# A graph layer with an expert layer on Trainium2: dividing, turning and measuring final node tiles between the last edge batches

## The chip, the cores and the metric

The kernel runs on one core of a Trainium2 chip. The metric is the device time of one execution in microseconds. The kernel before took 1845.05 us, the median of three runs from 1842.29 to 1846.93.

## The reference

`x` is 6250 nodes by 256. `src` and `dst` hold 106250 edges, sorted by `dst`, self-loops among them. What is computed, shortened:

```python
def _L0_gnn_ref(x, edge_index, W, att_src, att_dst, bias, gamma, beta):
    xh = (x @ W).reshape(N, H, D)
    e = leaky_relu(a_src[src] + a_dst[dst], 0.2)
    e = exp(e - segment_max(e, dst)[dst])
    alpha = e / segment_sum(e, dst)[dst]
    out = segment_sum(xh[src] * alpha[:, :, None], dst).reshape(N, H * D) + bias
    out = (out - mean(out, axis=0)) * rsqrt(var(out, axis=0) + 1e-5) * gamma + beta
    return out + x
...
x = x + _L0_gnn_ref(_layernorm(x), edge_index, ...)
x = x + _L0_ffn_ref(_layernorm(x), Wr, br, ln_g, ln_b, W1, b1, W2, b2)   # 8 experts, top 2
```

The kernel sums the weighted messages and the weights of a node side by side and divides once per node. The norm needs mean and variance of every column over all 6250 nodes, so nothing behind it starts before the last node is known.

## The kernel before

**Tiles.** 6250 nodes are `NT` = 49 tiles of 128 (the last has 106). `acc` in SBUF holds for each tile 256 sums and 8 weight sums (`ROW` = 264). The edges are cut into `USED` = 464 slots of 256 edges (`COUPLE` = 2 tiles of 128), each for one node tile; `SB` = 4 slots are a batch and there are `BATCHES` = 116. A node tile n is final when `CT` + n slots (`CT` = 416) have been added, whatever the data.

**One edge batch b.** GpSimd gathers rows of `node_table` by indirect DMA (L1230), eight gathers of 128 rows to a tile batch, 832 in all, into a ring of `GB` = 4; it waits until the messages of the rows that it overwrites are made. SyncE turns landed gathers into `rows_landed` (L1451) and loads the target rows (L1437). VectorE scores the batch (`score`, L1272 to L1282), sums the picks of the next (L1259), and then makes a message (L1290) and adds an older slot to `acc` (L1254) in turn, four times; adds run `ADDS_BEHIND` = 3 slots behind. ScalarE, once the batch is scored, makes two exponentials (L1418, L1423), the one-hot tile `onehotT` of batch b+2 (L1389, L1383) and the one-hot tile `onehot` of batch b+1 (L1397, L1383). TensorE multiplies the one-hot tile with the messages, four products a slot (L1372), and then makes the picks of batch b+2 (L1348). Ahead of each batch's products and between its slots it runs 16 products on a spare bank, `keep_clock` (L1337). Batches 4 to 99 also carry the splitting of the expert weights.

**Division.** In groups of 7 tiles, as soon as a group is final: VectorE takes the reciprocal of the weight sums (L1307) and, for the first five groups, multiplies (L1244, `multiply`). Groups 5 and 6 are multiplied by GpSimd behind its last gather. The first five divisions lie behind batches 106, 107, 109, 111 and 113.

**The norm.** Behind the last batch TensorE transposes `acc` in 13 chunks of four tiles (`CHUNK`; the last has one tile), eight transposes of 128x128 to a chunk (L1606), into three pairs of PSUM banks in turn (`TURNS`). VectorE takes bn_stats of each half chunk (L1546), ScalarE copies it back to `acc` turned (L1621). Then VectorE aggregates and works out scale and shift (L1553 to L1576); from L1564 on it needs `stage3_rows`, five loads that SyncE issues behind `wait_edges`, which waits for the last add, among others (L1521 to L1524, `bias`, `gamma`, `beta`, `x_logits`, `br`, with the loads of x into `r_ring`, L2096, around them). `wait_edges` also stands ahead of the copies of ScalarE and ahead of the iotas and memsets of GpSimd (L1638 to L1666), which VectorE needs at L1568. TensorE runs 20 `keep_clock` products, spreads the shift (L1611, L1612), runs 8 more and starts x1 (L1997, L2000), tile by tile, with VectorE (L1680, L1685) and ScalarE (L1530, L2036) behind it. Route, rows and the experts follow.

Each engine works through its own instructions in the order of the code; between engines only semaphores order the work.

## Time and profile before

| | |
|---|---|
| median of three runs | 1845.05 us |
| the profiled execution | 1842.22 us, span 1840.3 us |
| mean granted clock of TensorE | 0.943 |
| busy: TensorE, VectorE, ScalarE, GpSimd | 90%, 71%, 62%, 63% of the span |
| score of batch 105, 115 | starts at 1040.8, 1134.3 us |
| last add to `acc` | ends at 1143.0 us |
| the 26 bn_stats of the norm | 1143.4 to 1158.2 us |
| first x1 product | 1165.3 us |
| first expert product | 1252.5 us |

Times of a trace count from the span's start. The profile gives the busy time of each engine, groups of instructions by line, the waits with what ended them, the timeline, and the chain of work that ended last, followed back from the last instruction. PE is TensorE's matmuls and PEld its weight loads, DVE is VectorE, ACT ScalarE, POOL GpSimd, SP SyncE (SPq its DMA issues and waits). A granted clock of 1.00 is 2.4 GHz, 0.50 is 1.2 GHz.

### The profile page before, as it was taken

The page shows a single profiled execution, that of the slowest core. Times are in us where ns is not written, and L with a number is a line of the kernel's source. Part 1 is how long each engine was busy: PE and PEld are TensorE (multiplying, and loading weights), DVE is VectorE, ACT ScalarE, POOL GpSimd, SP SyncE. Part 2 cuts the span into 40 slices and gives each one's busy share as a digit, 9 for nine tenths or more (in the row PEclk, how much of TensorE's full clock was granted, in tenths as well). Part 3 has the DMA queues.
Part 4 walks back from the last instruction along what each step waited for, and adds up shares of the span by engine and source line. Part 5 has one row for each costly group of instructions (what it writes and reads, how often), then busy time and mean ns, then how long its engine had stood idle before and what let it go on. Part 6 is the DMA issues. An engine that isn't in the chain of part 4 may idle for free. (4 is left out here: it accounts for less than half of the span.)

```text
span 1840.3 us, 38213 instructions
## 1 busy us (share of the span) xinstructions
PE 1652.0 (90%) x11100; PEld 1228.8 (67%) x11100; DVE 1300.6 (71%) x3391; ACT 1150.2 (62%) x2503; POOL 1160.1 (63%) x1086
## 2 busy tenths in 40 slices
PE   6588979899897989999899879938999999999997
PEld 4445656566565656665665546717989999999996
DVE  6675858778685876867688768996666666666664
ACT  3665858788695976878697756863444343443443
POOL 1277777777777777777777776004666666556643
PEclk9888979999897998999899989959999999999998
DMA  8645555645555554555655444772333333323322
GB/s 298 226 125 146 146 165 146 170 124 165 151 148 166 144 154 135 155 160 150 167 148 146 124 113 122 257 304 71 54 51 48 49 53 51 51 48 51 51 42 33
DMA packets 122669, 235.10 MB, mean 128 GB/s; under 512 B 23452, under 2 KB 83112, under 8 KB 121288
## 3 DMA queue, kind: packets, MB, share of 16 engines
q0 software_dynamic: 60288, 141.01, 32.6%
q1 hardware_dynamic: 53276, 81.89, 13.4%
q10 hardware_dynamic: 8908, 9.75, 1.6%
q8 instruction: 103, 1.69, 0.4%
q14 instruction: 94, 0.77, 0.1%
HBM read 189.96 MB, written 43.44 MB: 127 GB/s over the span
## 5 line engine op out<-in xcount | busy, mean ns | idle before, releaser
L1230 POOL DMA_INDIRECT gather_ring<-node_table,src_tile x832 | 794.3, 955 | 261.6 <-issue 239.8
L1372 PE MATMUL bank<-message_ring,onehot 128*128 128x264 f32 x1856 | 509.6, 398 | 35.5 <-DVE message_ring L1290 35.5
L1337 PE MATMUL bank<-ones 128*128 128x512 bf16 x1900 | 511.8, 393 | 32.8 <-ACT message_ring L1423 20.7
L1372 PEld LDWEIGHTS bank<-message_ring,onehot 128*128 128x128 f32 x1856 | 356.4, 195 | 160.3 <-DVE message_ring L1290 68.7
L2366 POOL DMA_INDIRECT out_rows<-y,token_idx x105 | 203.9, 1942 | 215.9 <-DMA out_rows<-y,token_idx 156.4
L1337 PEld LDWEIGHTS bank<-ones 128*128 128x128 bf16 x1900 | 181.1, 100 | 219.7 <-issue 50.9
L1290 DVE TENSOR_TENSOR message_ring<-gather_ring,bank 128x512 f32<-128x512 f32 x464 | 315.4, 680 | 3.7 <-ACT bank L1418 1.1
L2334 ACT ACTIVATE hid<-bank,cols 128x256 f32<-128x256 f32 (+1 forms) x448 | 210.4, 551 | 147.3 <-PE bank L2274 144.4
L2274 PE MATMUL bank<-xe,w_hi 128*128 128x256 f16 (+1 forms) x1792 | 283.2, 266 | 0.9 <-DVE xe L2196 0.6
L1397 ACT ACTIVATE onehot<-iota_free,neg_dst 128x128 f32<-128x128 f32 x928 | 282.0, 386 | 0.5 <-PE bank L1372 0.5
L2291 PE MATMUL bank<-w,hid_hi 128*128 x1680 | 278.2, 273 | 0.0
L2274 PE MATMUL bank<-xe,w_lo 128*128 128x256 f16 (+1 forms) x896 | 235.5, 266 | 0.0
L2291 PE MATMUL bank<-w,hid_lo 128*128 x840 | 229.0, 273 | 0.0
L2344 POOL DMA_INDIRECT xs<-x_rows,token_idx x105 | 141.3, 1346 | 117.4 <-DVE token_idx L1978 85.7
L1254 DVE TENSOR_TENSOR acc<-acc,bank 128x264 f32 x464 | 196.0, 422 | 8.7 <-PE bank L1372 8.4
L2205 DVE TENSOR_SCALAR hid_hi<-hid,cols 128x1024 f16<-128x1024 f32 (+1 forms) x112 | 90.2, 805 | 145.5 <-ACT hid L2334 145.3
L2274 PEld LDWEIGHTS bank<-xe,w_hi 128*128 x1792 | 168.5, 98 | 21.7 <-issue 1.7
L1389 ACT ACTIVATE onehotT<-dst_row,minus_one_up 128x1024 bf16<-128x1024 uint8 x116 | 132.2, 1139 | 80.8 <-DMA dst_row<-dst_rows 80.8
L2291 PEld LDWEIGHTS bank<-w,hid_hi 128*128 128x128 f16 x1680 | 164.3, 98 | 20.1 <-issue 0.8
L2318 ACT ACTIVATE xe<-bank 128x512 f16<-128x512 f32 (+1 forms) x56 | 32.0, 571 | 195.4 <-PE bank L2255 195.4
L2208 DVE SCALAR_TENSOR_TENSOR hid_lo<-hid,cols,hid_hi 128x1024 f16<-128x1024 f32 (+1 forms) x112 | 136.4, 1218 | 4.0
L1383 ACT ACTIVATE onehot<-onehot,ones 128x1024 f32<-128x1024 f32 x116 | 133.2, 1149 | 3.8
(336 smaller groups left out, 1771.6 us busy)
## 6 DMA issues: line engine op xcount, KB each, us to landing
stage<-in_L_ffn_W SPq DMA_DIRECT2D x16, 1024.0 KB, 6.0
dst_row<-dst_rows SPq DMA_DIRECT2D x116, 128.0 KB, 3.5
gather_ring<-node_table,src_tile POOLq DMA_INDIRECT x832
w_split<-w_out SPq DMA_DIRECT2D x32, 256.0 KB
w<-w_split SPq DMA_DIRECT2D x8, 1024.0 KB, 9.6
node_table<-acc ACTq DMA_DIRECT2D x24, 264.0 KB
r_ring<-in_x_lanes SPq DMA_DIRECT2D x7, 896.0 KB, 7.0
xt<-in_x_lanes SPq DMA_DIRECT2D x24, 256.0 KB, 4.8
```

What stands on the lines that cost most here:

```text
L1230: e.indirect_dma_start(out=gather_ring[:, t % GB, j, :], out_offset=None, in_=node_table, in_offset=bass.IndirectOffsetOnAxis(ap=src_tile[ ...
L1254: e.tensor_tensor(a, a, bank[AGG[s % len(AGG)]][:, 0:ROW].rearrange("p (a c) -> p a c", a=1), ALU.add).then_inc(added, 1)
L1290: e.tensor_tensor(message_ring[:, s % MR, :, 0:D].rearrange("p r (h d) -> p r h d", d=DH), row_at(b, j)[:, :, :, 0:D].rearrange("p a r (h ...
L1337: e.matmul(to[:, :].rearrange("p (k n) -> p k n", k=2), halves[:, 0:P], halves.rearrange("p (a n) -> p a n", a=1).broadcast_to([P, 2, 2 * ...
L1372: made = e.matmul(bank[AGG[s % len(AGG)]][:, 0:ROW], onehot[:, b % OHB, COUPLE * j + r, :], message_ring[:, s % MR, r, :], start=(r == 0), ...
L1397: made = e.activation(onehot[:, b % OHB, j, :], iota_free[:, :], ACT.Abs, bias=neg_dst[:, s, r:r + 1])
L2208: e.scalar_tensor_tensor(hid_lo[:, q, cs, 0:w], hid[:, i % HR, :, 0:w], col_of(s, HS_COL), hid_hi[:, q, cs, 0:w], ALU.mult, ALU.subtract). ...
L2274: made = e.matmul(to, m[:, k, expert, at:at + P].rearrange("p a m -> p (a m)"), xe[:, q, x_, 0:w], start=(k == 0 and n == 0), stop=(k == K ...
L2291: made = e.matmul(bank[YB[q]][:, i * D:(i + 1) * D], a[:, q, c, ts], w2[:, expert, b, c, :].rearrange("p a d -> p (a d)"), start=(c == 0 a ...
L2334: made = e.activation(hid[:, i % HR, c, 0:w], bank[HB[2 * h + c // 2]][:, c % 2 * PW:c % 2 * PW + w], ACT.Gelu, bias=col_of(s, B1_COL + h ...
L2344: e.indirect_dma_start(out=xs[:, t % XR, :], out_offset=None, in_=x_rows, in_offset=bass.IndirectOffsetOnAxis(ap=token_idx[:, t:t + 1], ax ...
L2366: e.indirect_dma_start(out=out, out_offset=bass.IndirectOffsetOnAxis(ap=token_idx[:, t:t + 1], axis=0), in_=y[:, s % 2, t - first_tile(s), ...
```

## The change

The 13 chunks are divided, transposed, measured and copied back in part between the last edge batches. `TURN_AT` = 106. Behind the adds of batches 105 to 115 VectorE divides chunks 0 to 10, one a batch, reciprocal and product, and behind the last add chunks 11 and 12 in one. TensorE transposes chunk c behind the products of batch 105 + c and ahead of the picks. VectorE measures it at the head of the next batch, ahead of the score; ScalarE copies it back at the end of its share of that batch. Chunks 0 to 10 use banks 6 and 5, chunk 11 banks 2 and 7, chunk 12 banks 0 and 1; `turn` of chunks 1 to 10 waits for the copies of the chunk before. Chunks 10, 11 and 12 are measured and copied behind the last batch. The `keep_clock` products of batches 105 to 115 go, and the 20 of the norm write to bank 4. GpSimd multiplies nothing more. `feat` moves to another place in SBUF.

```diff
--- before.py
+++ after.py
@@ -138,6 +138,10 @@
         scale = small.take("scale", [P, 3, NE], I32)
         unscale = small.take("unscale", [P, 3, NE], I32)
         exponent = small.take("exponent", [P, 3, NE], I32)
+
+        NG, CHUNK = 7, 4
+        CHUNKS = ceil_div(NT, CHUNK)
+        feat = small.take("feat", [P, KD, CHUNKS, 6])
...
@@ -943,7 +944,9 @@
         onehot_made, onehotT_made, picks_done, scored, weighed, messages, summed, added = (
             sem(n) for n in ("onehot_made", "onehotT_made", "picks_done", "scored", "weighed", "messages", "summed", "added"))
         inverted, normalised = sem("inverted"), sem("normalised")
-        POOL_DIVIDES = GROUPS - 2
+        chunk_turned, chunk_kept, chunk_measured = (sem(n) for n in ("chunk_turned", "chunk_kept", "chunk_measured"))
+        CHUNK_BANKS = ((6, 5),) * (CHUNKS - 2) + ((2, 7), (0, 1))
+        TURN_AT = BATCHES - (CHUNKS - 3)
         dst_row_loaded = [sem(f"dst_row_loaded{i}") for i in range(2)]
         scalar_order = Order(sem("scalar_order"))
...
@@ -968,7 +971,7 @@
         B1_AT = W_AT + EB * HEADS
         PEAK_AT = P
         COLUMNS_AT = UNIT_AT + UNIT_STEPS * (UNITS - 1) + TOP_AT + 1
-        assert UNIT_AT + UNIT_STEPS * UNITS + 1 < BATCHES
+        assert UNIT_AT + UNIT_STEPS * UNITS < TURN_AT
...
@@ -1190,11 +1193,17 @@
         def tiles(g):
             return slice(g * NG, (g + 1) * NG)
 
+        def tiles_in(c):
+            return range(c * CHUNK, min((c + 1) * CHUNK, NT))
+
+        def chunk_bank(c, k):
+            return bank[CHUNK_BANKS[c][k]]
+
         def slots_in(b):
             return range(b * SB, min((b + 1) * SB, USED))
 
-        def final_at(g):
-            return CT + (g + 1) * NG - 1
+        def final_at(c):
+            return CT + tiles_in(c)[-1]
...
@@ -1238,11 +1247,35 @@
         def weights(b):
             return bank[PICKS[b % 2]][:, W_AT:W_AT + EB * HEADS].rearrange("p (j h) -> p j h", h=HEADS)
 
-        def multiply(e, g):
-            e.wait_ge(inverted, g + 1)
-            rows = acc[:, tiles(g), 0:D].rearrange("p n (h d) -> p n h d", d=DH)
-            e.tensor_tensor(rows, rows, acc[:, tiles(g), D:ROW].rearrange("p n (h a) -> p n h a", a=1)
-                            .broadcast_to([P, NG, HEADS, DH]), ALU.mult).then_inc(normalised, 1)
+        def turn(e, c):
+            e.wait_ge(normalised, c + 1)
+            if c == 0:
+                e.wait_ge(lo_made, PIECES * UNITS)
+            elif c < CHUNKS - 2:
+                e.wait_ge(chunk_kept, KD * c)
+            elif c == CHUNKS - 2:
+                e.wait_ge(messages, USED)
+            else:
+                e.wait_ge(added, USED)
+            for k in range(KD):
+                for n in tiles_in(c):
+                    made = e.transpose(chunk_bank(c, k)[:, n % CHUNK * P:(n % CHUNK + 1) * P], acc[:, n, k * P:(k + 1) * P],
+                                       ident[:, :])
+            made.then_inc(chunk_turned, 1)
+
+        def measure(e, c):
+            e.wait_ge(chunk_turned, c + 1)
+            nodes = sum(rows_of(n) for n in tiles_in(c))
+            for k in range(KD):
+                e.bn_stats(feat[:, k, c, :], chunk_bank(c, k)[:, 0:nodes]).then_inc(chunk_measured, 1)
+
+        def keep_turned(e, c):
+            at = tiles_in(c)
+            for k in range(KD):
+                e.wait_ge(chunk_measured, KD * c + k + 1)
+                e.activation(acc[:, at[0]:at[-1] + 1, k * P:(k + 1) * P],
+                             chunk_bank(c, k)[:, 0:len(at) * P].rearrange("p (n m) -> p n m", m=P), ACT.Copy
+                             ).then_inc(chunk_kept, 1)
...
@@ -1302,23 +1335,25 @@
                     if j == SB // 2 - 1:
                         vector_weights_between(e, b)
-            def divide(g):
-                e.wait_ge(added, final_at(g))
-                e.reciprocal(acc[:, tiles(g), D:ROW], acc[:, tiles(g), D:ROW]).then_inc(inverted, 1)
-                if g < POOL_DIVIDES:
-                    multiply(e, g)
-
-            def divide_final(done):
-                while divided[0] < GROUPS and final_at(divided[0]) <= done:
-                    divide(divided[0])
-                    divided[0] += 1
-
-            divided = [0]
+            def divide(first, last):
+                e.wait_ge(added, final_at(last))
+                of = slice(tiles_in(first)[0], tiles_in(last)[-1] + 1)
+                e.reciprocal(acc[:, of, D:ROW], acc[:, of, D:ROW]).then_inc(inverted, 1)
+                rows = acc[:, of, 0:D].rearrange("p n (h d) -> p n h d", d=DH)
+                e.wait_ge(inverted, first + 1)
+                e.tensor_tensor(rows, rows, acc[:, of, D:ROW].rearrange("p n (h a) -> p n h a", a=1)
+                                .broadcast_to([P, of.stop - of.start, HEADS, DH]), ALU.mult
+                                ).then_inc(normalised, last - first + 1)
+
+            assert final_at(CHUNKS - 3) <= USED - ADDS_BEHIND < final_at(CHUNKS - 2)
+            assert final_at(0) <= TURN_AT * SB - ADDS_BEHIND
             ring_rows = gather_ring[:, :, :, :].rearrange("p g (q r) d -> p (g q) r d", r=COUPLE)
             e.wait_ge(acc_started, GROUPS)
             load_tiles(e, 0)
             sum_picks(0)
             for b in range(BATCHES):
+                if b >= TURN_AT:
+                    measure(e, b - TURN_AT)
                 score(b)
                 vector_weights(e, b)
                 if b == COLUMNS_AT:
@@ -1326,10 +1361,11 @@
                 if b + 1 < BATCHES:
                     sum_picks(b + 1)
                 messages_and_adds(b)
-                divide_final(slots_in(b)[-1] + 1 - ADDS_BEHIND)
+                if b + 1 >= TURN_AT:
+                    divide(b + 1 - TURN_AT, b + 1 - TURN_AT)
             for s in range(USED - ADDS_BEHIND, USED):
                 add(*divmod(s, SB))
-            divide_final(USED)
+            divide(CHUNKS - 2, CHUNKS - 1)
...
@@ -1360,11 +1396,13 @@
             for b in range(BATCHES):
                 if b == 0:
                     e.wait_ge(acc_started, GROUPS)
-                keep_clock(e, IDLE_PRODUCTS // 2, idle_bank)
+                if b + 1 < TURN_AT:
+                    keep_clock(e, IDLE_PRODUCTS // 2, idle_bank)
                 e.wait_ge(onehot_made, b + 1)
                 e.wait_ge(weighed, 2 * b + 2)
                 for j, s in enumerate(slots_in(b)):
-                    keep_clock(e, IDLE_PRODUCTS // 2 // SB, idle_bank)
+                    if b + 1 < TURN_AT:
+                        keep_clock(e, IDLE_PRODUCTS // 2 // SB, idle_bank)
                     e.wait_ge(messages, s + 1)
                     if s >= len(AGG):
                         e.wait_ge(added, s - len(AGG) + 1)
@@ -1373,6 +1411,8 @@
                                         message_ring[:, s % MR, r, :], start=(r == 0), stop=(r == COUPLE - 1))
                     made.then_inc(summed, 1)
                 tensor_peaks(e, b)
+                if b + 1 >= TURN_AT:
+                    turn(e, b + 1 - TURN_AT)
                 if b + 2 < BATCHES:
                     picks(b + 2)
...
@@ -1429,6 +1469,8 @@
                 if b + 1 < BATCHES:
                     make_onehot(b + 1)
                 scalar_weights(e, b, 1)
+                if b >= TURN_AT:
+                    keep_turned(e, b - TURN_AT)
...
@@ -1499,8 +1540,7 @@
         TOTALS, RANKED, LISTED = range(1, 4)
         w2_ready, b2_loaded = sem("w2_ready"), sem("b2_loaded")
         RANK, TOT, LIST, SEGMENTS = 5, 6, 7, 4
-        TURNS = (PICKS, (0, 1), (3, 4))
-        TURN_RING, X1_RING, SPREAD = len(TURNS), 6, 6
+        X1_RING, SPREAD = 6, 6
...
@@ -1530,23 +1570,10 @@
             e.activation(r_ring[:, g % RB, n % NG, :], r_ring[:, g % RB, n % NG, :], ACT.Identity,
                          bias=x_shift[:, n:n + 1], scale=rstd[:, n:n + 1]).then_inc(resid_made, 1)
 
-        def tiles_in(c):
-            return range(c * CHUNK, min((c + 1) * CHUNK, NT))
-
-        def chunk_bank(c, k):
-            return bank[TURNS[c % TURN_RING][k]]
-
         def vector_norm(e):
+            for c in range(CHUNKS - 3, CHUNKS):
+                measure(e, c)
             wait_edges(e)
-
-            def measure(c):
-                e.wait_ge(chunk_turned, c + 1)
-                nodes = sum(rows_of(n) for n in tiles_in(c))
-                for k in range(KD):
-                    e.bn_stats(feat[:, k, c, :], chunk_bank(c, k)[:, 0:nodes]).then_inc(chunk_measured, 1)
-
-            for c in range(CHUNKS):
-                measure(c)
 
...
@@ -1593,20 +1620,10 @@
             vector_order.of(e.tensor_tensor(tok16[:, :], tok_in_block[:, 0:NT], valid[:, :], ALU.mult))
 
         def tensor_norm(e):
-            for c in range(CHUNKS):
-                e.wait_ge(normalised, tiles_in(c)[-1] // NG + 1)
-                if c == 0:
-                    e.wait_ge(messages, USED)
-                if c == 1:
-                    e.wait_ge(added, USED)
-                if c >= TURN_RING:
-                    e.wait_ge(chunk_kept, KD * (c - TURN_RING + 1))
-                for k in range(KD):
-                    for n in tiles_in(c):
-                        made = e.transpose(chunk_bank(c, k)[:, n % CHUNK * P:(n % CHUNK + 1) * P], acc[:, n, k * P:(k + 1) * P],
-                                           ident[:, :])
-                made.then_inc(chunk_turned, 1)
-            keep_clock(e, 20, idle_bank)
+            for c in (CHUNKS - 2, CHUNKS - 1):
+                turn(e, c)
+            keep_clock(e, 20, bank[AGG[-1]])
+            e.wait_ge(chunk_kept, KD * CHUNKS)
             e.wait_ge(shift_unit_made, KD)
             e.matmul(bank[SPREAD][:, 0:ACROSS], ones[:, :], shifted_unit[:, 0, :], start=True, stop=False)
             e.matmul(bank[SPREAD][:, 0:ACROSS], ones[:, :], shifted_unit[:, 1, :], start=False, stop=True
@@ -1614,18 +1631,10 @@
...
             keep_clock(e, 8, idle_bank)
 
         def scalar_norm(e):
-            def keep(c):
-                at = tiles_in(c)
-                for k in range(KD):
-                    e.wait_ge(chunk_measured, KD * c + k + 1)
-                    e.activation(acc[:, at[0]:at[-1] + 1, k * P:(k + 1) * P],
-                                 chunk_bank(c, k)[:, 0:len(at) * P].rearrange("p (n m) -> p n m", m=P), ACT.Copy
-                                 ).then_inc(chunk_kept, 1)
-
             e.activation(table_seed[:, :], ones[:, 0:1], ACT.Sqrt)
             wait_edges(e)
-            for c in range(CHUNKS):
-                keep(c)
+            for c in range(CHUNKS - 3, CHUNKS):
+                keep_turned(e, c)
             e.wait_ge(var_known, 1)
             e.activation(sd_col, var_col, ACT.Sqrt, bias=eps[:, :]).then_inc(sd_made, 1)
             for n in range(RESID_AHEAD):
...
@@ -2386,8 +2395,6 @@
             pool_first_edges(e)
             general_path(e, max_moves)
             pool_edges(e, range(GB, TILE_BATCHES))
-            for g in range(POOL_DIVIDES, GROUPS):
-                multiply(e, g)
             pool_iotas(e)
             pool_ffn(e)
```

## Rows read from the trace of the kernel before

**Rows 1.** The chain that ended last, in order of time: start us, length us, what.

```profile
1142.39 0.89 PE bank L1606 x8
...
1143.42 14.79 DVE feat L1546 x26
...
1158.23 0.48 DVE agg L1553
```

**Rows 2.** Waits of 1040 to 1143 us: who waited for whom, us, times, longest.

```profile
DVE zbuf L1272 <- SPq L1451: 17.1, 5, 5.2
...
POOL gather_ring L1230 <- issue: 21.0, 69, 0.3
```

**Rows 3.** VectorE's timeline, 1020 to 1137: start us, us, engine line, what [idle before].

```profile
1040.81 0.17 DVE L1272 TENSOR_TENSOR zbuf<-gather_ring,picked 128x16 f32<-128x16 f32 x1
...
1048.05 0.79 DVE L1272 TENSOR_TENSOR zbuf<-gather_ring,picked 128x16 f32<-128x16 f32 x4
...
1079.27 1.03 DVE L1272 TENSOR_TENSOR zbuf<-gather_ring,picked 128x16 f32<-128x16 f32 x4 [3.81 <-SPq L1451]
...
1085.37 0.50 DVE L1307 RECIPROCAL acc<-acc 128x56 f32<-128x56 f32 x1
...
1085.90 2.03 DVE L1244 TENSOR_TENSOR acc<-acc 128x1792 f32<-128x1792 f32 x1
...
1134.32 1.02 DVE L1272 TENSOR_TENSOR zbuf<-gather_ring,picked 128x16 f32<-128x16 f32 x4 [1.90 <-SPq L1451]
```

**Rows 4.** ScalarE's timeline, 1050 to 1137.

```profile
1119.68 0.21 ACT L1418 ACTIVATE bank<-zbuf 128x64 f32<-128x64 f32 x1
...
1124.65 1.15 ACT L1383 ACTIVATE onehot<-onehot,ones 128x1024 f32<-128x1024 f32 x1
...
1136.16 0.23 ACT L1418 ACTIVATE bank<-zbuf 128x64 f32<-128x64 f32 x1 [4.55 <-DVE zbuf L1282]
```

**Rows 5.** Groups of instructions of 1142.9 to 1158.3, shapes apart: xcount | busy us, mean ns.

```profile
L1546 DVE BATCH_NORM_STATS2 feat<-bank 128x6 f32<-128x512 f32 x24 | 14.4, 682 | 0.0
...
L1621 ACT ACTIVATE acc<-bank 128x512 f32<-128x512 f32 x24 | 14.3, 598 | 6.1 <-DVE feat L1546 6.0
```

**Rows 6.** Timeline of all engines, 1128 to 1168.

```profile
1142.22 2.82 PE L1606 MATMUL bank<-ident,acc 128*128 128x128 f32 x24
...
1142.53 0.43 DVE L1254 TENSOR_TENSOR acc<-acc,bank 128x264 f32 x1 [0.88 <-PE bank L1372]
...
1147.10 0.47 SPq L1524 DMA_DIRECT2D br_row<-in_L_ffn_br  x1
...
1154.60 0.20 POOL L1666 MEMSET all_ones<- 128x128 f16 x1
...
1159.92 0.15 DVE L1564 TENSOR_TENSOR bn_cols<-bn_cols 128x2 f32<-128x2 f32 x1
```

**Rows 7.** GpSimd's timeline, 1020 to 1137.

```profile
1086.17 2.58 POOL L1230 DMA_INDIRECT gather_ring<-node_table,src_tile  x1 [0.30 <-issue]
...
1130.16 0.95 POOL L1230 DMA_INDIRECT gather_ring<-node_table,src_tile  x1 [0.30 <-issue]
```

**Rows 8.** TensorE's timeline, 1030 to 1137.

```profile
1030.65 0.59 PE L1337 MATMUL bank<-ones 128*128 128x512 bf16 x2 [3.18 <-ACT message_ring L1423]
...
1071.80 1.01 PE L1337 MATMUL bank<-ones 128*128 128x512 bf16 x2 [4.27 <-ACT message_ring L1423]
...
1072.61 1.96 PE L1372 MATMUL bank<-message_ring,onehot 128*128 128x264 f32 x4
...
1076.81 0.60 PE L1337 MATMUL bank<-ones 128*128 128x512 bf16 x2
...
1093.33 0.68 PE L1337 MATMUL bank<-ones 128*128 128x512 bf16 x2 [4.06 <-ACT message_ring L1423]
```

**Rows 9.** The tile br_row: from the issue of its load to landing.

```profile
DMA to landing us min/median/max: 8.5/8.5/8.5
```

**Rows 10.** Windows: from:to, us, busy us (xcount) of each engine, PEclk, DMA share, GB/s.

```profile
1146.00:1156.00 10.00, 8.95 (x69) 7.14 (x67) 10.00 (x18) 9.99 (x17) 8.49 (x26) 1.00 0.88 346
```

6 lines of the change are left out of this document (1 added, 5 removed).

## The prediction

> **What bounds the kernel now.** I read the chain of waits first, then the waits of the last edge batches, then the timelines of the single engines there. In the chain [rows 1] the reader is to see that the 26 bn_stats of L1546 lie on the path for 14.79 us between the last edge batch and the norm: that is what the change attacks. Ahead of them stand 116 edge batches. The waits of their last stretch [rows 2] say what paces those: VectorE stands still for 17.1 us in five waits for gathered rows (the release comes through SyncE at L1451), while GpSimd waits for nothing but the 0.3 us of issue between two gathers. So in batches 108 to 111 and in 115 the gathers of GpSimd set the pace, and VectorE and ScalarE have gaps. Batches 105 to 107, 113 and 114 have the rows in time. Score(105) starts at 1040.81 and score(115) at 1134.32 [rows 3]: ten batches in 93.5 us, 9.35 us each.
>
> All times are those of the profiled execution, 1842.22 us (span 1840.3 and 1.9 around it); the median of the runs shown is 1845.05, 2.8 more. I work out a difference on the first and add it to the median.
>
> **The change part by part.**
>
> *The wait ring that it makes.* With c = b - 105, the code of batch b is then: VectorE scores b, makes messages and adds, divides chunk c; TensorE does the products of b, then turn(c); VectorE measures chunk c at the head of batch b+1, ahead of score(b+1). Turn(c) waits for chunk_kept of chunk c-1, because chunks 0 to 10 all use the one pair of banks (6, 5), and keep_turned(c-1) stands last in ScalarE's batch b, behind both one-hot tiles. And ScalarE's batch b begins with the exponentials that need score(b). This closes a ring: score(b), ScalarE's whole batch b, keep, turn, measure, score(b+1). Nothing in it can run ahead, so its length is a floor for the batch, whatever the gathers do. Queued behind the waits are: on VectorE the scoring of the next batch, on TensorE picks(b+2), on ScalarE nothing.
>
> *Its length*, from rows. Score start to ScalarE's first exponential: 1134.32 to 1136.16, 1.84 us [rows 3, 4]. From there through the exponentials, onehotT and onehot where ScalarE works without a gap: 1119.68 to 1125.80, 6.12 us [rows 4]. Two copies of 512 columns: 598 ns each [rows 5], a little overlapped, 1.1. Eight transposes: in the chain they end 0.89 us after 1142.39 [rows 1], and the first starts at 1142.22 [rows 6]; with the weight load ahead 1.3 to 1.4, and a semaphore on each side 0.1. Two bn_stats at 0.6 us a piece (14.79 / 26 = 0.57, the last two short) 1.2. Together 11.6; VectorE's scoring starts a little quicker behind other work, so I take 11.4 (bounds 11.1 and 11.8). In the kernel before ScalarE's one-hot tiles for b+1 can still be in the making while VectorE scores b+1; in the ring they can't, and so a batch is longer than both 9.35 and the ten microseconds that GpSimd needs for eight gathers.
>
> *The other way round the ring*, through VectorE: the last add ends 6.1 us behind the score start (from 1079.27 to the reciprocal at 1085.37 [rows 3]), then the division of four tiles. The reciprocal of 56 columns takes 0.50; of 32 I take 0.35. The product of seven tiles takes 2.03; of four between 1.16 (in proportion) and 1.3 (with a fixed part), taken 1.22. So divided at +7.65, turned and measured at +10.3. ScalarE's side is longer by 1.1 us. It rules where ScalarE has both one-hot tiles to make, batches 106 to 113.
>
> *Sum over the ten batches.* 105 to 106: its adds end about 1048.07, where score(106) starts now [rows 3], and division, turn and measure (1.57 + 1.4 + 1.2) push that to 1052.2: 11.4 us. Eight rings of 11.4: 91.2. Batch 114 makes no onehotT, so VectorE's side counts: 10.3. In all 112.9 against 93.5: **+19.4 us**, half a microsecond a batch either way for the bounds (-3 to +4). All rows have landed long before: the last gather ends at 1131.1 [rows 7] and score(115) comes at about 1153.7. The gathers may be held up by the ring of four buffers, but batch 111's messages are out at about 1115, ahead of the last eight gathers, which take the ten microseconds up to 1131.1.
>
> *The keep-clock products* of batches 105 to 115 go: 16 a batch, bf16 and 512 columns. TensorE's own work is then some 5.5 us in 11.4, with a pause of about 3.8 us between the picks and the next message and 2.3 more ahead of the turn. The trace has the clock at half after pauses of 4.27 and 4.06 us and at full after 3.18 [rows 8]. At half everything takes about twice its time (two keep-clock products 1.01 instead of 0.59, the four products of a slot 1.96), and in the case of 1071.80 the work ran so until two products took 0.60 again at 1076.81 [rows 8], five microseconds; the products of a batch then end 0.6 to 1.4 us later than the copies that turn(c) waits for anyway. I take that the turn is late for it in about two batches, by 0.5 us: +1.0 (bounds 0 and +12, every batch with its turn late too). The pauses fall in a part that hides most of it; without that cover, four slots at half clock cost 4 us a batch (half of 4 x 1.96).
>
> *The last batch.* Now the last add ends at 1142.96, 8.64 us behind score(115), and it waited 0.88 for TensorE [rows 6], whose keep-clock products stood in between. That wait goes; the division of chunk 10 (1.57) comes in front of the last three adds: 8.64 - 0.88 + 1.57 = 9.33; with a part of the products at half clock I take 9.8. **+1.2 us** (+0.6 to +2.5).
>
> *Behind the last add.* VectorE divides five tiles (0.4 + 1.5), measures chunk 10, 11 and the short 12 while TensorE turns them, and has the statistics at about 4.9 us behind the last add; now the 26 bn_stats end 15.3 behind it (1158.23 [rows 1] against 1142.96). So ten would be won if nothing else came late. But L1564 waits for stage3_rows, five loads that SyncE issues only when the last add is done. The last of them is issued at 1147.10 [rows 6] and takes 8.5 us to land [rows 9]: 1155.6, 12.64 behind the last add, and nothing in the change moves these loads with respect to it. L1564 runs now at 1159.92 [rows 6], 16.96 behind it. So the stage gives back 16.96 - 12.7: **-4.3 us**, not ten. GpSimd's two products (3.2 us each) go, and its iotas, 8 us long and done now at 1154.8 [rows 6], would be done 8 to 10 us behind the last add: covered by the loads, and worth 1 to 2 us if those were not there.
>
> *TensorE ahead of x1.* The 20 products of keep_clock then end about 8 us behind the last add and the spread product comes at 14.7: a pause of over 6 us. So the spread, the 8 products behind it (0.59 for two at full clock, 1.01 and more at half [rows 8]) and the first x1 tiles run at half: **+1.7 us** (0 to +3).
>
> Sum: 19.4 + 1.0 + 1.2 - 4.3 + 1.7 = **+19.0**: 1845.05 + 19.0 = **1864.0 us**.
>
> **Two rules weighed.** GpSimd's gather that comes up while VectorE multiplies in acc is held: 2.58 us instead of 0.95, ending 0.82 us behind the product's end [rows 3, 7]; the five such in the stretch take 1.76, 2.07, 2.58, 2.61 and 1.62, together 5.9 us over 0.95 each. The Trainium skill, "SBUF — State Buffer", section "Who interferes with whom", says that a VectorE product with two SBUF inputs and a GpSimd operation that reads SBUF exclude each other for the whole instruction; by that rule, the trace agrees. With four tiles a product is shorter but there are ten: about 0.6 us each, 6 again; it matters only in the rival where the gathers still rule. In the stretch of 98 transposes the granted clock stays at 1.00 [rows 10], full level. The Trainium skill, "TensorE: Matmul & The Clock Gate", section "Part 4: PE-mode transpose", says that transposes don't count as busy and don't engage the full clock; here the trace speaks against it. What it would do is rival C.
>
> **The rivals.**
> A, the forecast: the ring through ScalarE. +19.0.
> B, only the ring through VectorE: the copies come early enough (ScalarE's batch is shorter than I read, or turn doesn't wait for them). Then nine batches at 10.2 and the first at 11.4: 103.2 against 93.5, +9.7; with the same ends +8.8: 1854. For it: only 1.1 us lie between the two sides. Against it: the order of the code and the 6.12 us.
> C, TensorE stays at half clock through the last ten batches, since the turns and the fp32 products don't bring it back: turn(c) at +11.4, ring 15: +33 more, 1894. Against it: at 1071.80 to 1077 steady work brought it back [rows 8].
> D, the other side: VectorE's 17.1 us of waiting for rows swallow the added work (ten measures of 1.2 and 10 divisions of 1.57, less the 13 us of division that are there now: 15 us). Decided by whether turn and copies run within the waits; then score(115) stays: 0.7 - 4.3 + 1.7 = -1.9, 1843. If the loads of stage 3 land sooner too, up to -8: 1837. Against it: the waits lie in five batches, and the ring needs 11.4 in all ten.
>
> **How the numbers follow.** A 0.72, B 0.10, C 0.07, D 0.11 (0.07 within 0.3%, 0.04 beyond). 0.3% is 5.5 us, about what a measurement of this kernel can tell from no change. The likeliest lies within 1857 to 1873 by its bounds; the range that holds 8 in 10 takes in B and a part of the clock's cost: 1853 to 1877. Slower 0.89, same 0.07, faster 0.04.
>
> **What would show it.** Score starts in batches 106 to 113 of the new profile 11.4 us apart, VectorE waiting there for TensorE's transposes ahead of bn_stats and no longer for rows; TensorE's transposes released by ScalarE's copies into acc; the last add near 1163; three chunks measured within 5 us behind it; L1564 some 12.7 us behind it, ready long before; granted clock under 1 in part of the last ten batches and ahead of x1. It would be wrong if rows still end VectorE's waits (D), if the division and not the copy releases the transposes (B), or if the products of the batches stay at twice their time (C).

## The result and the profile after

The kernel before took 1843.19 us (median of five runs, 1841.09 to 1846.93), the changed one 1864.23 us (five runs, 1862.45 to 1867.51): a ratio of 1.0109, 95% interval 1.0092 to 1.0125. The predicted time was 1864.0 us. The profiled execution has a span of 1862.4 us, 22.1 more than that of before. The forecast met the time, but two of its terms were off by some 4 and 6 us in opposite directions, so the ledger matters more here than the total. It also started from 1845.05, the median of three runs, 1.86 above the median of five: forecast was +19.0 us, measured +21.0.

**The last ten batches.** VectorE's timeline of batch 110 (start us, length us, engine, line, operation, output<-input, and in brackets the idle time ahead and what ended it), between two scores, L1305; answers to [rows 3]:

```profile
1099.30 0.41 DVE L1305 TENSOR_TENSOR zbuf<-gather_ring,picked 128x16 f32<-128x16 f32 x4
...
1104.64 0.35 DVE L1341 RECIPROCAL acc<-acc 128x32 f32<-128x32 f32 x1
1105.03 1.23 DVE L1344 TENSOR_TENSOR acc<-acc 128x1024 f32<-128x1024 f32 x1
1108.88 1.30 DVE L1270 BATCH_NORM_STATS2 feat<-bank 128x6 f32<-128x512 f32 x2 [2.63 <-PE bank L1262]
1110.09 0.54 DVE L1305 TENSOR_TENSOR zbuf<-gather_ring,picked 128x16 f32<-128x16 f32 x4
```

ScalarE's timeline of the same batch; answers to [rows 4]:

```profile
1100.52 0.23 ACT L1458 ACTIVATE bank<-zbuf 128x64 f32<-128x64 f32 x1 [3.69 <-DVE zbuf L1315]
...
1105.51 1.15 ACT L1423 ACTIVATE onehot<-onehot,ones 128x1024 f32<-128x1024 f32 x1
1106.57 1.06 ACT L1276 ACTIVATE acc<-bank 128x512 f32<-128x512 f32 x2
1111.44 0.23 ACT L1458 ACTIVATE bank<-zbuf 128x64 f32<-128x64 f32 x1 [3.81 <-DVE zbuf L1315]
```

TensorE's timeline of the same batch; answers to [rows 8]:

```profile
1101.83 5.49 PE L1410 MATMUL bank<-message_ring,onehot 128*128 128x264 f32 x16 [3.58 <-DVE message_ring L1323]
1107.78 1.06 PE L1262 MATMUL bank<-ident,acc 128*128 128x128 f32 x8 [0.46 <-ACT acc L1276]
1108.68 0.57 PE L1384 MATMUL bank<-pick_parts,onehotT 128*128 x8
```

The reader is to follow the ring through the three: score at 1099.30, ScalarE's first exponential at 1100.52, its last copy done at 1107.63, transposes from 1107.78, their end lets bn_stats start at 1108.88, and the next score comes at 1110.09. That is 1.22 + 7.11 + 1.25 + 1.21 = 10.79 us. The waits of 1040 to 1162 (who waited for whom: us in total, times, longest), which answer to [rows 2]:

```profile
DVE feat L1270 <- PE bank L1262: 25.4, 10, 3.3
...
PE bank L1262 <- ACT acc L1276: 4.8, 6, 2.0
...
PE bank L1262 <- DVE acc L1344: 0.7, 1, 0.7
```

The five waits for gathered rows [rows 2] are gone; in their place stand ten waits for transposes, 25.4 us, so the ring is closed in all ten. The transposes themselves waited for ScalarE's copies in six batches and for the division in one; in the others they followed the batch's products without a wait. Score(105) starts at 1044.13, score(115) at 1153.98: 109.85 us for ten batches, against 93.51.

**The clock.** Windows of one batch each (from:to, us, busy us and count of PE, PEld, DVE, ACT, POOL, granted clock, DMA share, GB/s):

```profile
1044.00:1055.00 11.00, 8.13 (x53) 6.06 (x51) 8.27 (x21) 8.13 (x18) 8.56 (x9) 1.00 0.49 122
...
1110.00:1121.00 11.00, 6.70 (x32) 5.27 (x32) 8.28 (x21) 7.05 (x15) 8.56 (x9) 0.84 0.48 124
1121.00:1132.00 11.00, 7.90 (x32) 6.32 (x32) 7.52 (x21) 7.14 (x16) 8.56 (x9) 0.69 0.38 101
1132.00:1143.00 11.00, 5.17 (x32) 3.97 (x32) 8.32 (x22) 7.04 (x15) 1.48 (x2) 1.00 0.17 35
```

Full level (2.4 GHz) is 1.00, half (1.2 GHz) 0.50; a mean of 0.84 is a batch with half the clock for a third of its time. TensorE's timeline has the two extremes:

```profile
1123.58 6.83 PE L1410 MATMUL bank<-message_ring,onehot 128*128 128x264 f32 x16 [3.62 <-DVE message_ring L1323]
...
1135.06 3.91 PE L1410 MATMUL bank<-message_ring,onehot 128*128 128x264 f32 x16 [3.59 <-DVE message_ring L1323]
```

In most of batches 106 to 115 the 16 products took 5.2 to 5.9 us (5.49 four times), in two, at 1079.71 and 1123.58, 6.58 and 6.83, and in one, at 1135.06 and wholly at full clock, 3.91. The pauses ahead of them, 3.38 to 3.78 us, hardly differ. Batch 113, the one at full clock, is as long as the others, 10.79 us: it is not the clock that makes the batches long.

**Behind the last add**, which ends at 1162.57. Timeline of all engines, 1160 to 1190; answers to [rows 6]:

```profile
1162.14 0.43 DVE L1287 TENSOR_TENSOR acc<-acc,bank 128x264 f32 x1 [0.23 <-PE bank L1410]
...
1162.95 0.70 POOL L1654 MEMSET part_rows<- 1x128 bf16 x3
...
1164.52 2.92 DVE L1270 BATCH_NORM_STATS2 feat<-bank 128x6 f32<-128x512 f32 x6
...
1166.29 0.49 SPq L1564 DMA_DIRECT2D br_row<-in_L_ffn_br  x1
...
1174.93 0.81 POOL L1647 IOTA iota_e<- 128x392 f32 x1 [11.28 <-issue]
1174.96 0.16 DVE L1591 TENSOR_TENSOR bn_cols<-bn_cols 128x2 f32<-128x2 f32 x1 [5.61 <-DMA br_row<-in_L_ffn_br]
...
1181.69 0.20 POOL L1675 MEMSET all_ones<- 128x128 f16 x1
1181.98 0.17 DVE L1595 RECIPROCAL bn_cols<-bn_cols 128x2 f32<-128x2 f32 x1 [6.67 <-POOL all_ones L1675]
...
1183.54 1.22 PE L1628 MATMUL bank<-shifted_unit,ones 128*128 128x264 f32 x2 [13.26 <-DVE shifted_unit L1600]
...
1188.30 0.28 PE L2006 MATMUL bank<-shift_parts,part_rows 128*128 128x264 bf16 x1
```

The six bn_stats that are left end 4.9 us behind the last add, where 26 ended at 15.3. But nothing downstream comes sooner by that: L1591 waits 5.61 us for br_row, and then L1595, the reciprocal of the scale, waits 6.67 us for GpSimd. GpSimd had stood still for 11.28 us between its memsets and its first iota, released by nothing that the profile shows ("issue"). So the reciprocal of the scale comes 19.41 us behind the last add (before: 17.51), and the first x1 product, L2006, 25.73 (before: 22.33). In the kernel before the same reciprocal, L1568, waited for ScalarE alone (VectorE's timeline of before):

```profile
1160.47 0.17 DVE L1568 RECIPROCAL bn_cols<-bn_cols 128x2 f32<-128x2 f32 x1 [0.20 <-ACT bn_cols L1630]
```

The chain of waits shows the same time as path:

```profile
1162.14 0.44 DVE acc L1287
1163.71 11.22 issue
1174.93 0.81 POOL iota_e L1647
```

**The ledger** of the 22.1 us between the two profiled executions: up to score(105) +3.3, score(105) to score(115) +16.3, from there to the last add 0.0, to the reciprocal of the scale +1.9, to x1 +1.5, from x1 to the end -0.9. The first and the last lie outside of what the change touches; runs of one kernel differ by up to 5.8 us. The four others are +19.7, the medians differ by 21.0.

### The profile page after: what moved, and what is told of

The parts are those of the page before. It is cut to its first block, busy times and chain, and to the rows that moved or that the text cites. A ratio compares the mean times of both kernels' runs of the same rounds, so it can differ in the third digit from the quotient of the medians.

```text
span 1862.4 us, 37874 instructions
## 1 busy us (share of the span) xinstructions
PE 1628.7 (87%) x10924; PEld 1222.9 (66%) x10924; DVE 1302.0 (70%) x3403; ACT 1146.1 (62%) x2503; POOL 1151.5 (62%) x1084
## 3 DMA queue, kind: packets, MB, share of 16 engines
q1 hardware_dynamic: 53276, 81.89, 13.4%
## 4 chain that ended last, share of the span: by engine, by line
PE 57%; POOL 11%; DMA 9%; issue 8%; DVE 7%; ACT 6%; DVEq 1%; SPq 1%; POOLq 0%; ACTq 0%
PE bank L2283 14%; PE bank L2300 14%; PE bank L1410 12%; POOL gather_ring L1239 10%; PE bank L1373 9%; DMA stage<-in_L_ffn_W 4%; PE bank L1051 3%; DMA gather_ring<-node_table,src_tile 2%; ACT onehot L1437 2%; DVE message_ring L1323 2%; PE bank L795 1%; ACT acc L2062 1%; PE bank L2264 1%; DMA out_rows<-y,token_idx 1%; ACT onehotT L1429 1%
## 5 line engine op out<-in xcount | busy, mean ns | idle before, releaser
L1410 PE MATMUL bank<-message_ring,onehot 128*128 128x264 f32 x1856 | 515.7, 406 | 71.8 <-DVE message_ring L1323 71.6
L1410 PEld LDWEIGHTS bank<-message_ring,onehot 128*128 128x128 f32 x1856 | 363.6, 199 | 195.9 <-DVE message_ring L1323 67.1
L1373 PE MATMUL bank<-ones 128*128 128x512 bf16 x1724 | 462.4, 393 | 18.8 <-DVE acc L739 11.9
L1373 PEld LDWEIGHTS bank<-ones 128*128 128x128 bf16 x1724 | 164.3, 100 | 187.3 <-issue 32.7
L1458 ACT ACTIVATE bank<-zbuf 128x64 f32<-128x64 f32 x116 | 25.9, 223 | 187.5 <-DVE zbuf L1315 187.2
```

Source lines behind the costliest of these rows:

```text
L1373: e.matmul(to[:, :].rearrange("p (k n) -> p k n", k=2), halves[:, 0:P], halves.rearrange("p (a n) -> p a n", a=1).broadcast_to([P, 2, 2 * ...
L1410: made = e.matmul(bank[AGG[s % len(AGG)]][:, 0:ROW], onehot[:, b % OHB, COUPLE * j + r, :], message_ring[:, s % MR, r, :], start=(r == 0), ...
```

## The experiments

The runs below are from three chips: e1 to e4 from one, e5 to e8 from a second, e9 to e11 from a third. On all three the edge batches of every kernel are longer than in the first result, and the kernel before takes 2338, 2326 and 2341 us. VectorE there stops irregularly, in the last ten batches up to 13 us at a time, on waits that the trace only calls "remote" (85 of them, 540 us, in the trace of e7_after_again; none in the two traces of the first result). So what is compared is the ratio to the kernel before on the same chip, good to about 0.3%, 7 us, and, more finely, stretches of the traces. The changed kernel itself was run again on the second chip only; for the first of the three, e1_seed stands in for it, since its edge batches have the same code. A batch is called undisturbed where no such wait lies in it. Whatever an expectation gives as a whole time or as the length of the ten batches holds for batches without these stops; against it stand the undisturbed batches and the stretch behind the last add. One stretch can be set side by side for every kernel, with "reciprocal" for that of the scale:

| kernel | ratio to before, 95% interval | score(105) to last add, us | reciprocal behind last add | x1 behind last add |
|---|---|---|---|---|
| before, first chip | | 102.2 | 17.5 | 22.3 |
| changed, first chip | 1.0109 [1.0092, 1.0125] | 118.4 | 19.4 | 25.7 |
| e9_before_again | 0.9989 [0.9955, 1.0024] | 124.8 | 17.5 | 22.3 |
| e7_after_again | 1.0075 [1.0046, 1.0104] | 142.5 | 19.9 | 26.0 |
| e1_seed | 1.0069 [1.0034, 1.0104] | 142.7 | 12.8 | 19.1 |
| e2_keep_early | 1.0111 [1.0039, 1.0183] | 138.7 | 19.8 | 25.8 |
| e3_measure_late | 1.0026 [0.9992, 1.0061] | 131.7 | 20.5 | 26.7 |
| e8_late_again | 1.0045 [1.0015, 1.0076] | 129.3 | 19.9 | 26.8 |
| e5_late_seed | 0.9985 [0.9960, 1.0010] | 129.1 | 12.1 | 18.8 |
| e6_late_seed_loads | 0.9968 [0.9943, 0.9993] | 129.4 | 8.2 | 13.3 |
| e11_best_again | 0.9994 [0.9960, 1.0028] | 130.3 | 8.2 | 13.1 |
| e4_vector_divides | 1.0036 [1.0005, 1.0067] | 112.8 | 20.3 | 25.1 |
| e10_no_keep_clock | 1.0017 [0.9980, 1.0054] | 124.6 | 17.5 | 22.3 |

Three theories: R, the ring costs the ten batches; S, a start-up pause of GpSimd, which the edge batches used to cover, costs the stretch behind the last add; against R the rivals that VectorE's own added work or the half clock costs them.

**Theory S: a small iota behind the last gather.** e1_seed is the changed kernel with

```diff
             pool_edges(e, range(GB, TILE_BATCHES))
+            e.iota(pool_seed[:, :], [[1, 8]], base=0, channel_multiplier=0, allow_small_or_imprecise_dtypes=True)
             pool_iotas(e)
```

> The changed kernel with one small iota (8 columns, into a tile of its own, read by nobody) on GpSimd directly behind its last gather, ahead of the wait for the edges. Theory S: GpSimd pays some 7 to 11 us once when it goes over from gathers to an iota or a product (the kernel before: 7.33 us, under the last batches, ahead of its product; the changed kernel: 11.28 us behind the last add, ahead of its first iota, on the path). Then here the small iota takes the pause under the last edge batches, iota_e starts less than 1 us behind the memsets, the iotas end about 8.2 us behind the last add, L1591 is released by the loads at 12.4 behind it and the reciprocal of scale comes 0.4 behind that and no longer 19.4: 6.5 us less on the path, less up to 1 us of half clock; time about 1858. Rival: the pause belongs to the place, as GpSimd waits for SyncE's loads or for the bus that they fill; then it stays at 11 us and the time at 1864.

GpSimd's timeline of e1_seed:

```profile
1619.25 0.14 POOL L2399 IOTA pool_seed<- 128x8 f32 x1 [7.61 <-issue]
...
1648.33 0.70 POOL L1655 MEMSET part_rows<- 1x128 bf16 x3
1649.10 0.81 POOL L1648 IOTA iota_e<- 128x392 f32 x1
```

VectorE's timeline of e1_seed, the same stretch:

```profile
1647.52 0.43 DVE L1288 TENSOR_TENSOR acc<-acc,bank 128x264 f32 x1 [0.23 <-PE bank L1411]
...
1660.38 0.16 DVE L1592 TENSOR_TENSOR bn_cols<-bn_cols 128x2 f32<-128x2 f32 x1 [5.67 <-DMA br_row<-in_L_ffn_br]
...
1660.78 0.17 DVE L1596 RECIPROCAL bn_cols<-bn_cols 128x2 f32<-128x2 f32 x1
```

The iotas follow the memsets at once. The pause, 7.61 us, has moved ahead of the small iota, where GpSimd has nothing else to do. The reciprocal comes 12.8 us behind the last add (1647.95), right behind br_row, the predicted bound: 6.6 to 7 us less, and x1 with it. S is shown by these stretches; the whole time doesn't resolve it, since the ratio of 1.0069 is known to 0.35% only. The rival, that the pause belongs to its place, is refuted: at the same place there is none now. S was to be read in the trace of before as well, where the same pause stood ahead of GpSimd's first product behind the gathers, hidden (GpSimd's timeline of before, not among the rows of the prediction):

```profile
1138.43 3.20 POOL L1244 TENSOR_TENSOR acc<-acc 128x1792 f32<-128x1792 f32 x1 [7.33 <-issue]
```

**Theory R, one side of the ring: copies ahead of the one-hot tiles.** e2_keep_early, the changed kernel with

```diff
                 made.then_inc(weighed, 1)
+                if b >= TURN_AT:
+                    keep_turned(e, b - TURN_AT)
                 if b + 2 < BATCHES:
                     make_onehotT(b + 2)
...
                 scalar_weights(e, b, 1)
-                if b >= TURN_AT:
-                    keep_turned(e, b - TURN_AT)
```

> The changed kernel with ScalarE's copies of a chunk moved from the end of its batch to directly behind the two exponentials, ahead of both one-hot tiles. Theory A (ring through ScalarE): turn no longer waits for the copies; the ring then runs through VectorE's adds and division: 5.4 + 1.6 + 1.25 + 1.2 = 9.4 us where TensorE's products end in time, 10.6 where they run at half clock and the turn waits for them. So the score starts of batches 106 to 114 lie 9.4 to 10.6 us apart instead of 10.9 to 11.5, five to ten microseconds less in all: 1855 to 1859. Rival B (VectorE's side of the ring is the floor already): no change, 1864. Rival: onehotT and with it the picks come 1.1 us later and take the gain away.

Its intervals of score from 111 to 115, undisturbed, are 10.36, 10.19, 10.14 and 10.26 us; in e1_seed, on the same chip and with the edge batches of the changed kernel, the same four are 10.92, 11.26, 10.79 and 10.27 (e7_after_again, on another chip: 10.93, 11.52, 10.80 and 10.65). Batches 106 and 107 have no remote wait either and gained nothing: 10.85 and 11.41 against 10.89 and 11.42. Ten batches take 130.1 us for 134.2, 4.0 less: just short of the five to ten that were expected. TensorE's timeline of batch 112:

```profile
1613.33 5.49 PE L1410 MATMUL bank<-message_ring,onehot 128*128 128x264 f32 x16 [3.63 <-DVE message_ring L1323]
1618.65 1.04 PE L1262 MATMUL bank<-ident,acc 128*128 128x128 f32 x8
```

The transposes now stand right behind the batch's own products, without a wait. In batches 111 to 113 the ring is shorter by 0.6 to 1.1 us, and it is closed by the products, partly at half clock; VectorE's division ends at 1617.75, 0.9 ahead of the transposes. So the copies alone were only a part of this side of the ring. The whole doesn't resolve 3 to 5 us (1.0111, a wide interval).

**Theory R, the ring open: measure behind the adds.** e3_measure_late, the changed kernel with

```diff
-                if b >= TURN_AT:
-                    measure(e, b - TURN_AT)
                 score(b)
...
                 messages_and_adds(b)
+                if b >= TURN_AT:
+                    measure(e, b - TURN_AT)
```

> The changed kernel with the bn_stats of a chunk moved from ahead of the score to behind the messages and adds of the same batch. The ring is open: score(b+1) doesn't wait for turn. Theory A: the batches go back to the gathers' pace, score(105) to score(115) 93 to 97 us instead of 109.9, 13 to 16 us less; behind the last add nothing changes (19.4 to the reciprocal): 1848 to 1852. Rival: the work itself (division, bn_stats, copies, transposes) and not the waiting fills the batches; then it stays within 3 us of 1864. Rival C (half clock is the cost): no change either, as TensorE's work is the same.

VectorE's timeline of batches 113 and 114 in the second run of this kernel, e8_late_again:

```profile
1598.80 0.43 DVE L1305 TENSOR_TENSOR zbuf<-gather_ring,picked 128x16 f32<-128x16 f32 x4
...
1600.60 0.56 DVE L1292 TENSOR_REDUCE picked<-bank 128x128 f32<-128x384 f32 x1 [0.59 <-PE bank L1384]
...
1607.67 0.60 DVE L1305 TENSOR_TENSOR zbuf<-gather_ring,picked 128x16 f32<-128x16 f32 x4
...
1616.08 0.43 DVE L1305 TENSOR_TENSOR zbuf<-gather_ring,picked 128x16 f32<-128x16 f32 x4
```

The first run of this kernel (1.0026) has undisturbed intervals of 8.71, 8.87 and 9.08 us, and a pause of 12.37 us ahead of the iotas, with the reciprocal 20.5 behind the last add: the gain lies in the batches alone, S is untouched. On the same chip as e1_seed its score(105) to last add is 131.7 us for 142.7. Above stand 8.87 and 8.41 us for two batches that divide and measure a chunk each: VectorE's whole added work is in them, 8.1 us busy, and TensorE keeps the pauses and has no keep_clock. In the changed kernel the same two are 10.80 and 10.65 (e7_after_again, the same chip as e8). Of the other batches, 107 and 112 are undisturbed in both: 9.27 and 10.21 for 10.81 and 11.52. That is 1.3 to 2.2 us a batch, 1.8 in the mean, for the order of two calls. The added work can't be what costs them, since it is still there; nor can the clock, since the changed kernel's batch 113 takes 10.8 us at full clock too. The last batch is 1.2 us longer with the ring open (9.8 for 8.6 us), because bn_stats now stand ahead of the last adds. With 8.1 us of work VectorE itself is the next floor. 

> The changed kernel with only the ring open (measure of chunk c behind the adds of the next batch instead of ahead of its score), without the small iota. Theory R: score(105) to score(115) 90 to 97 us, that is 13 to 19 under the changed kernel, while behind the last add GpSimd's pause of 11 us stays and the reciprocal of the scale comes 19 to 20 behind the last add: 1845 to 1851 where the changed kernel takes 1864. Rival V (VectorE's own work): within 3 us of the changed kernel. The difference to the kernel with ring open and small iota is the price of the pause alone: 6 to 7 us.

> The changed kernel itself, unchanged, beside the two kernels with the ring open. Expected as in its first profile: score starts of batches 106 to 115 10.8 to 11.5 us apart, 109 to 110.5 us in all; GpSimd stands still for 11 us behind its memsets; the reciprocal of the scale 19 to 20 us behind the last add; 19 to 22 us over the kernel before (ratio 1.010 to 1.012) on a chip where that takes 1843.

Score(105) to score(115) takes 133.9 us in the changed kernel, 119.5 with the ring open: 14.4 less, within the 13 to 19 expected; to the last add it is 13.2 less. The medians differ by 6.8 us only (2341.07 and 2334.30), below the expectation; each is known to about 7 us. For e7_after_again the undisturbed batches, the pause (11.72 us) and the reciprocal (19.9) came as expected; the ratio 1.0075 is smaller than expected and than the first chip's: 15.5 us over the kernel before. Why stays open. That the ring lies beside some of the long stops there would fit, but the stretches don't show it: 142.5 against 124.8 us (e9_before_again, another chip) is no smaller a difference than the first chip's 118.4 against 102.2.

**Both, and the loads.** e5_late_seed has the two edits of e3_measure_late and e1_seed. e6_late_seed_loads adds

```diff
             wait_edges(e)
+            stage3_loads(e)
             for g in range(RB):
                 load(g)
-                if g == 2:
-                    stage3_loads(e)
```

> The changed kernel with two edits together: VectorE measures chunk c behind the adds of the next batch and not ahead of its score (the ring is open), and GpSimd makes one small iota of 8 columns into a spare tile behind its last gather (its pause then lies under the edge batches). Theory R+S (the ring costs the ten batches, GpSimd's pause the stretch behind the last add): score(105) to score(115) 90 to 97 us instead of 109.85; the reciprocal of the scale 12.6 to 13.2 us behind the last add instead of 19.4, released by br_row's landing; first x1 product 19 to 20 behind the last add instead of 25.7. Together 20 to 26 us under the changed kernel of the same chip: on a chip where that takes 1864, 1838 to 1844, so 0 to 5 under the kernel before. Rival V (not the ring but VectorE's own added work, ten divisions and ten measures, costs the ten batches): they stay at 105 to 110 us, and only 6 to 7 us are won.

19.8 us less than the changed kernel, just under the 20 to 26 expected. The traces have 13.4 of it in the edge batches and 7.2 behind them. The reciprocal comes 12.1 and x1 18.8 us behind the last add, 0.5 and 0.2 sooner than expected: br_row landed 8.0 us after its issue here. Against e8_late_again, which has the ring open but no small iota, the reciprocal comes 7.8 us sooner, a little more than the 6 to 7 expected; the medians are 13.1 apart.

> As the kernel with the open ring and the small iota, and in addition SyncE issues the five loads of stage3_rows ahead of the first three loads of r_ring, and not behind them. Theory S2 (behind the last add the landing of br_row now ends the wait): the last of the five is issued 2.4 us behind the last add instead of 3.7, and lands 8 to 8.6 later: the reciprocal at 10.6 to 11.4 instead of 12.8 behind the last add, 1.3 to 2.2 us under the kernel without this edit, so 1836 to 1843 where that takes 1838 to 1844. Rival: the loads land as late as before since the queues are full of gathered-row or w2 packets, or the x rows in r_ring then come late for x1: no change or up to 2 us more.

A timeline of all engines of e6_late_seed_loads, its last add ending at 1619.77:

```profile
1621.77 0.43 SPq L1565 DMA_DIRECT2D br_row<-in_L_ffn_br  x1
...
1627.34 0.26 DVE L1592 TENSOR_TENSOR bn_cols<-bn_cols 128x2 f32<-128x2 f32 x1
...
1627.98 0.17 DVE L1596 RECIPROCAL bn_cols<-bn_cols 128x2 f32<-128x2 f32 x1 [0.20 <-POOL all_ones L1676]
...
1629.84 0.61 PE L1629 MATMUL bank<-shifted_unit,ones 128*128 128x264 f32 x2
```

And the tile br_row in this kernel; answers to [rows 9]:

```profile
DMA to landing us min/median/max: 3.3/3.3/3.3
```

More than expected. The load is issued 1.7 us sooner with respect to the last add (2.0 instead of 3.7), near what was expected, and lands 3.3 us later instead of 8.0 (e5_late_seed): that was the mistake in the expectation, which kept the 8 to 8.6 us. VectorE's statistics and GpSimd's iotas and memsets now end 7.6 and 8.1 us behind the last add, the loads at 5.3, and x1 starts 13.3 us behind the last add instead of 25.7. TensorE's pause is short enough here for the spread to run at full clock (0.61 instead of 1.22 us). 2315.18 us, 0.9968 of the kernel before, interval 0.9943 to 0.9993.

> The changed kernel with all three edits (ring open, small iota behind the last gather, loads of stage3_rows ahead of those of r_ring), again. On a chip where the edge batches run as in the first profile: score(105) to score(115) 90 to 97 us, the last add 9.8 behind, the reciprocal of the scale 8.2 and the first x1 product 13.3 behind the last add (as in its first trace), which is 9 us less than in the kernel before; with 1 us more in the last batch the whole is 6 to 11 us under the kernel before if the ten batches cost 91 to 95. Elsewhere ratio 0.994 to 0.999 as in its first run (0.9968). Rival: measuring and dividing cost VectorE's batches as much as the norm gives back, ratio 1.000 or more.

The stages behind the last add repeat to 0.2 us, but the ratio is 0.9994, just above the 0.994 to 0.999 expected, with 1.0 inside its interval. From the traces this version loses 4.6 to 5.5 us against e9_before_again up to the last add and wins 9.0 to 9.2 behind it: about 4 us, 0.2%, and that lies between the two ratios. So it beats the changed kernel by 0.8 to 1.1% (0.9994 and 0.9968 against 1.0075); that it beats the kernel before is likely but not settled.

**The kernel before, for its trace.**

> The kernel before, unchanged, for its trace beside the others of the same chip. On a chip where the edge batches take as in the first profile: score(105) to score(115) 93.5 us, the last add 8.6 behind score(115), the reciprocal of the scale 17.5 and the first x1 product 22.3 us behind the last add. On a chip where the edge batches stop for landed rows, the ten batches take 105 to 120 us, and the two figures behind the last add are the same to within 1 us.

The two figures behind the last add are those of the first chip (17.49, 22.3), so that stretch can be compared across chips. The last add came 11.2 behind score(115), not 8.6; score(115) itself had come only 5.9 behind score(114).

**One part alone: no keep_clock.** e10_no_keep_clock is the kernel before with

```diff
-                keep_clock(e, IDLE_PRODUCTS // 2, idle_bank)
+                if b < BATCHES - 11:
+                    keep_clock(e, IDLE_PRODUCTS // 2, idle_bank)
...
-                    keep_clock(e, IDLE_PRODUCTS // 2 // SB, idle_bank)
+                    if b < BATCHES - 11:
+                        keep_clock(e, IDLE_PRODUCTS // 2 // SB, idle_bank)
```

> The kernel before without the keep_clock products of batches 105 to 115, that edit of the change alone. Theory: the granted clock drops to half in the pauses of 3 to 5 us that are left open in most of these batches, but the batch products catch up ahead of what they are waited for by: the ten batches stay within 1.5 us of the kernel before, the last add comes 7.8 to 8.6 behind score(115) (the wait of 0.88 for TensorE there goes or halves). Total within 0.1% of before. Rival C (half clock persists and is on the path): four slots at half clock cost up to 4 us a batch, so up to 40 us over the kernel before.

TensorE's timeline of its batches 113 and 114:

```profile
1603.17 5.49 PE L1374 MATMUL bank<-message_ring,onehot 128*128 128x264 f32 x16 [4.61 <-DVE message_ring L1290]
1608.49 0.36 PE L1348 MATMUL bank<-pick_parts,onehotT 128*128 x8
1611.15 3.80 PE L1374 MATMUL bank<-message_ring,onehot 128*128 128x264 f32 x16 [2.30 <-DVE message_ring L1290]
```

Behind a pause of 4.61 us the batch takes 5.49 us, behind 2.30 us 3.80. The granted clock over the stretch is 0.75, with the products (e9_before_again) 0.85. Yet the ten batches take 112.7 us against 113.6, and score(105) to the last add 124.6 against 124.8: nothing of the 1.7 us a batch shows in the total. The expectation for the last add behind score(115) was missed (11.9 us; the kernel before has 11.2 on this chip): in batch 115 VectorE waited 1.10 and 0.46 us for TensorE, where the kernel before waited 0.89. The rival with its 40 us is refuted; 1 or 2 us either way, beside stops of up to 13, are not resolved.

**One part alone: VectorE divides.** e4_vector_divides is the kernel before with

```diff
-        POOL_DIVIDES = GROUPS - 2
+        POOL_DIVIDES = GROUPS
```

> The kernel before with one thing changed: VectorE multiplies groups 5 and 6 too, GpSimd none. Nothing is interleaved. Theory S: the pause of GpSimd comes behind the last add, 7 to 11 us, and its iotas end 16 to 19.5 us behind the last add instead of 11.8; the reciprocal of scale comes now 17.5 behind it, so 0 to 2 us are added; with the product of group 6 on VectorE ahead of the bn_stats (2.0 us, under which TensorE can't start chunk 10) and the one of group 5 in the last batches: 1843 to 1848. Rival (no pause where only iotas follow): the iotas end 8 behind the last add and the time stays at 1843 to 1845.

VectorE's timeline of e4_vector_divides has the reciprocal at 1638.74, 20.3 us behind the last add, where the kernel before has 17.5: one product of 2.0 us and the bn_stats queued behind it. GpSimd, now without its product, met its pause (11.14 us) at the iotas, and they end 19.2 behind the last add, just covered by the bn_stats. So this part alone costs 2.8 us in the norm, 0.8 more than expected, and already brings the pause behind the last add; it is only the shorter norm of the change that makes the pause the last thing. Its ratio, 1.0036, is some 8 us, more than the norm's 2.8; the interval begins at 1.0005, and the rest stays open. Its edge stretch (112.8 us) has one long stop fewer than the others and says nothing.

## Why the prediction was right, point by point

**The ring** was right in mechanism: each of its four hand-overs is in the trace, in the order of the prediction, and opening it at one place gives 1.3 to 2.2 us a batch back. Its length was 10.9 us instead of 11.4 (the terms written down add up to 11.7, not 11.6, and were taken down to 11.4). The term mis-sized is the first, score start to ScalarE: 1.84 us was read from 1134.32, a score that stood behind a wait for rows and whose four adds took 1.02 us [rows 3]; behind bn_stats the four take 0.41 to 0.56 and the term is 1.22 to 1.37. The rest held: 7.11 against 6.12 + 1.1, transposes 1.25 against 1.3 to 1.4 and a semaphore, bn_stats 1.21 against 1.2. Batch 114 took 10.66 for 10.3, since its products, not the division, held the turn. Ten batches: +16.3 instead of +20.4 with the clock.

**The keep_clock products**: +1.0 predicted, the turn late in about two batches by 0.5. It was late in two, at 11.37 and 11.52 us for 10.9: +1.1. It was close to being more. In batch 110 the products end 0.3 us ahead of the copies, so without the copies as cover (e2_keep_early) they are the bound.

**The last batch**: +1.2 predicted, -0.05 measured (8.59 us for 8.64). The step that failed laid the division of 1.57 us in front of the last adds. They wait for TensorE's last products all the same (the last add waited 0.23 for them), and the division lies beside those.

**Behind the last add**: the loads bound L1591 at 12.4 us, predicted 12.7. That the gain is not ten but about four at this place was right. What failed is the sentence that the iotas "would be done 8 to 10 us behind the last add: covered by the loads". They are 8 us long, but start 12.4 us behind it. The cost of a GpSimd instruction was counted from its own rows, and the idle time of 7.33 us with nothing to release it, ahead of the first product behind the gathers, was passed over as free because it lay beside other work. The change takes the cover away: -4.3 became +1.9, 6.2 us. e1_seed gives 6.6 of it back.

**TensorE ahead of x1**: +1.7 predicted for the half clock, +1.5 measured (reciprocal to x1 6.3 us for 4.8).

**The sum**: +19.0 predicted, +19.7 in the parts touched. Ring and last batch together 5.3 us too much, GpSimd's pause 6.2 too little: the closeness of 1864.0 is luck in the second half, and the range was earned by the ring. Rival B (10.2 us a batch through VectorE) is what e2_keep_early comes to in batches 111 to 114, but through TensorE's products; its +8.8 is a slip of half a microsecond, since 9.7 with the same ends is +9.3. C is refuted: the mean clock of no batch is below 0.69, and no batch is longer than 11.5 us. D is refuted by its own sign: none of VectorE's waits in the ten batches is for rows.

What stays open: why the medians differ by 1.3 us more than the touched parts; what the "remote" waits of the other three chips are; and what a kernel with the ring open takes on the first chip, since it was not run there.

## What to carry to other kernels

When independent work is woven into a loop that runs over several engines, write down who waits for whom from one turn to the next: if the new piece sits at the head of an engine's turn and needs the end of another's, it closes a ring, and the sum around it, not anyone's busy time, is the new period; one call moved behind the engine's own work opens it. Before counting a hidden engine's work as covered in its new place, read also the idle time ahead of it that nothing releases: that goes with the work, and may grow. Where a stage is shortened, list everything that ends it, with times from its start (here statistics 4.9, loads 12.4, iotas and memsets 19.3 us), since only taking them all down moves the end.
